# Attention and experts: shared weights added once to all 16 experts, experts' sums fetched per step from DRAM, values and experts' columns trimmed from 64 to 47

## The chip, the cores and the metric

The kernel runs on one core of one Trainium2 chip. The metric is the device time in microseconds (us). The engines of the core are TensorE (PE; its weight loads are PEld), VectorE (DVE), ScalarE (ACT), GpSimd (POOL) and SyncE (SP), which here only issues transfers. They run their own instruction streams and wait for each other by semaphores.

## The reference

64 images of 64x64x3 pass through a spectral network, which gives 64 tokens of width 64 per image; 77 text tokens per image are embedded and put behind them. So each image has 141 tokens. Then:

```
h = h + attention(layernorm(h))          # 8 heads of 8, mask: 7x7 neighbourhood on a grid of 11
h = h + ffn(layernorm(h))
# ffn, per image, with e = route_id[image]:
f = relu(x @ Wi.T + bi)                  # 64 -> 128
for l in range(2):
    shared = f @ Ws[l].T + bs[l]
    routed = f @ Wr[l, e].T + br[l, e]   # one of 16 experts
    f = relu(shared + routed + f)
out = f @ Wo.T + bo                      # 128 -> 64
```

The change lies in the attention and in this last network alone. All is float32.

## The kernel before

`token_network` makes the tokens and writes them to DRAM (about 2645 of the 3238 us). `attention_and_experts` then takes them two images (a pair) at a time, 32 pairs. The 141 tokens of an image are three blocks of BLK = 47 queries (b0, b1, b2), each against KEYS = 119 keys. The two images of a pair lie on partitions 0 to 46 and 64 to 110, so tiles have 64 slots an image of which 47 are used.

Each engine has its own written-out order of work, `step(i, p, b)`, called for each couple i, pair p of it and block b by `each_step`: couples 0 and 1 unrolled, a loop over the middle ones, the last one and a drain unrolled. `at(i, p, b, lag)` gives the work item that lies `lag` blocks back; in one step three pairs are in progress: `here` (scores, mask, softmax, values), `prev` one pair behind (output of attention, residual, second layer norm) and `old` two pairs behind (the network with the experts). `num(i, p)` is the pair's number.

The work of a step, by engine:

- TensorE: `turn` (transposes of the softmax, L1775), `back_o` (L1800), `back_layer` (both layers of the experts, L1829), `back_out` (L1836), `scores` (L1764), `front1` (L1735), `values` (softmax times values, L1788), `back_y` (L1815), `front2` (L1742, L1743), `back_in` (input matmul, L1820), `front3` (L1750), `back_proj` (projection, L1806). In block b1's part of the order stand: turn of b0, back_o, layer 0, scores of b2, values of b0, front3, back_proj, layer 1.
- VectorE: `with_mask` (scores + mask, PSUM to SBUF, L2015), `row_max` (L2025), `norm_end` (L1998), `o_norm` (L2031, L2034), `weights` (L2055), `residual` (L2043), `norm` (L1985 to L1994), `final` (L2064).
- GpSimd: `shift` (subtracts the row's maximum, L2124), `keys` (L2118), `power` (L2107, L2109), `with_bias` (L2131).
- ScalarE: `exp` (L1907), copies out of PSUM (L1886 to L1921), ReLUs (L1925, L1931).
- SyncE: tokens of pairs ahead (`xs`, `xr`, L1691) and results out (L1716).

`weights` stands in VectorE's order in block b1 of the step, between the row maximum of b1 and the mask addition of b2. For each of the two images it reads the image's expert number into a register and adds the shared weights `ws` (the identity for "+ f" is put into them once, L2072) to that expert's slice of `wr`, which holds all 16 in SBUF, [128, 2 layers, 16 experts, 129]; 128 weights and a bias. The sum goes to `wc[p]`. `wc_ready` lets TensorE begin layer 0 of that pair a step later.

The values are matmuls with the transposed softmax stationary, 64 columns an image of which 47 are queries, and 9 moving columns a head (8 values and a column of ones for the sum). Input matmul, layers and output matmul also run over all 64 slots an image.

Of the kernel before, what the change touches and what calls it, by code (L numbers as in the profile page):

```python
# [1545 lines left out]
BLK = TOK // 3  # L1546
# [8 lines left out]
def attention_and_experts(nc, t, tokens, out):  # L1555

    with ExitStack() as ctx:
# [58 lines left out]
        p_ps = ps[0:KEYS, 2:4, :]  # L1616
        o_ps = ps[:, 4, 0:3 * HEADS * (HD + 1)]
        fr_ps = [ps[:, 5, :], ps[:, 6, :]]
        ff_ps = ps[:, 7, :]
# [44 lines left out]
        f_ready = sem("f_ready")  # L1664
        wc_ready = sem("wc_ready")
        y_psr = sem("y_psr")
# [17 lines left out]
        def _(sp):  # L1684
# [13 lines left out]
            sp.wait_ge(t_setup, 4)  # L1698

            def step(i, p, b):  # L1700
                if b == 0 and at(i, p, 0, 0):
# [5 lines left out]
                if b == 0 and at(i, p, 0, 0) and (c := at(i, p, 0, -6)):  # L1707

                    sp.wait_ge(xn_ready, num(i, p) + 1)
                    waits_apart(sp, t_passed)  # L1710
                    load(xs[p], c[0], c[1], xs_in[p])
                if b == 0 and (c := at(i, p, 0, 9)):
                    sp.wait_ge(fin_ready, num(c[0], c[1]) + 1)
                    waits_apart(sp, t_passed)
                    for m in range(2):
                        sp.dma_start(out[bass.ds(2 * num(c[0], c[1]) + m, 1)].rearrange("a (b r) d -> (a r) b d", b=3),  # L1716
                                     fin[c[1]][64 * m:64 * m + BLK]).then_inc(fin_out[c[1]], 16)
# [5 lines left out]
        def _(pe):  # L1723
            pe.wait_ge(t_const, 16 * len(loads))
            pe.wait_ge(t_zero, 4)
            pe.wait_ge(t_setup, 6)
# [52 lines left out]
            def values(i, p, b):  # L1779
# [5 lines left out]
                for h in range(HEADS):  # L1785
                    for m in range(2):
                        o = (HEADS * b + h) * (HD + 1)
                        last = nc.tensor.matmul(o_ps[64 * m:64 * m + 64, o:o + HD + 1],  # L1788
                                                pT[:, h, 64 * m:64 * m + 64], vv[p][:, m, b, h, :],
                                                start=True, stop=True)  # L1790
# [27 lines left out]
            def back_in(i, p):  # L1818
                pe.wait_ge(yT_ready, num(i, p) + 1)
                nc.tensor.matmul(ff_ps[:, 0:384], wi[:], yT[:].rearrange("d b n -> d (b n)"),  # L1820
                                 start=True, stop=True).then_inc(f_psr, 1)

            def back_layer(i, p, l):
                g = num(i, p)
                pe.wait_ge(f_ready, 3 * g + l + 1)
                if l == 0:
                    pe.wait_ge(wc_ready, g + 1)
                for m in range(2):
                    last = nc.tensor.matmul(ff_ps[:, 192 * m:192 * m + 192], wc[p][:, l, m, 0:HID], ff[l][:, :, m, :],  # L1829
                                            start=True, stop=True)  # L1830
                last.then_inc(f_psr, 1)

            def back_out(i, p):
                pe.wait_ge(f_ready, 3 * num(i, p) + 3)
                for b in range(3):
                    last = nc.tensor.matmul(ff_ps[:, 64 * b:64 * b + 64], ff[2][:, b].rearrange("k m n -> k (m n)"), wo[:],  # L1836
                                            start=True, stop=True)
                last.then_inc(y_psr, 1)
# [39 lines left out]
        def _(act):  # L1878
            act.wait_ge(t_zero, 4)
            act.wait_ge(t_const, 16 * len(loads))  # L1880
# [42 lines left out]
            def relu_in(i, p):  # L1923
                act.wait_ge(f_psr, 3 * num(i, p) + 1)
                nc.scalar.activation(ff[0][:].rearrange("k b m n -> k (b m n)"), ff_ps[:, 0:384], ACT.Relu, bias=bi[:]  # L1925
                                     ).then_inc(f_ready, 1)

            def relu_layer(i, p, l):
                act.wait_ge(f_psr, 3 * num(i, p) + l + 2)
                for m in range(2):  # L1930
                    last = nc.scalar.activation(ff[l + 1][:, :, m, :], ff_ps[:, 192 * m:192 * m + 192]  # L1931
                                                .rearrange("k (b n) -> k b n", b=3), ACT.Relu, bias=wc[p][:, l, m, HID:HID + 1])
# [33 lines left out]
        def _(dve):  # L1966
            for p in range(2):
                nc.vector.memset(xs[p][:], 0.0).then_inc(xs_zero, 1)
            for tile in (xT, qT[0], qT[1], yT):
                nc.vector.memset(tile[:], 0.0).then_inc(t_zero, 1)  # L1970
            for p in range(2):
                nc.vector.memset(vv[p][:, :, :, :, HD:HD + 1], 1.0).then_inc(t_setup, 1)
# [75 lines left out]

            def weights(i, p):

                g = num(i, p)
                at_least(dve, y_psr, g - 1)
                for m in range(2):
                    e = dve.value_load(route[0:1, bass.ds(4 * i + 2 * p + m, 1)], min_val=0, max_val=EXPERTS - 1)
                    last = nc.vector.tensor_tensor(wc[p][:, :, m, :], wr[:, :, bass.ds(e, 1), :].rearrange("p l a n -> p l (a n)"),  # L2055
                                                   ws[:], ALU.add)
                last.then_inc(wc_ready, 1)

            def final(i, p):
# [13 lines left out]
                                    ).then_inc(t_setup, 1)  # L2073
            dve.wait_ge(t_setup, 7)

            def step(i, p, b):
# [12 lines left out]
                if b == 0 and prev:  # L2089
                    o_norm(*prev[0:2])  # L2090
                if b == 1 and prev:
                    weights(*prev[0:2])
                if b == 2 and prev:
# [193 lines left out]
```

## Time and profile before

| | |
|---|---|
| time, median of 3 runs | 3235.67 us (3233.77 to 3237.13) |
| span of the profiled execution | 3238.3 us |
| TensorE matmul busy | 2941.1 us, 91% |
| VectorE busy | 2306.9 us, 71% |
| ScalarE busy | 2158.6 us, 67% |
| GpSimd busy | 2115.6 us, 65% |
| attention and experts | from about 2649 us to the end |
| mean granted clock of TensorE | 0.964 |

The span is the profiled execution's time from the first to the last instruction; no time around it is given beside it, so it is compared with the median of the timed runs, of another execution each. Matmuls are pipelined: an instruction's duration is longer than the distance to the next one's start, which is what a sequence of them costs. The granted clock is a share of 2.4 GHz: 1.00 is that, 0.50 is 1.2 GHz. In the lines, PE, PEld, DVE, ACT, POOL are the engines, "L1829" is a line of the kernel, `pst` the PSUM tensor of this stage and `sm`, `mx`, `wc` tiles.

### The profile page before, as it was taken

To read this page: it belongs to the slowest core of one execution; us is meant where nothing else is said; L and a number is where in the kernel's file an instruction comes from. 1 tells how busy PE (TensorE), PEld (TensorE's weight loads), DVE (VectorE), ACT (ScalarE), POOL (GpSimd) and SP (SyncE) were. 2 spreads that over 40 slices of the span, in tenths; PEclk is the share of its full clock that TensorE was granted. 3 is DMA by queue.
4 is the path that set the end of the run, shared out by engine and by line. 5 is a ranking of instruction groups with operands and counts; after the bars stand their busy time and mean duration, and the time that the engine had idled before them with its cause. 6 is when DMAs were issued, how large, how long until landed. Compare 5 with 4: busy or idle time off the path is not lost. (4 is left out here: it accounts for less than half of the span.)

```text
span 3238.3 us, 190683 instructions
## 1 busy us (share of the span) xinstructions
PE 2941.1 (91%) x80542; PEld 1998.9 (62%) x80542; DVE 2306.9 (71%) x3829; ACT 2158.6 (67%) x3644; POOL 2115.6 (65%) x1147
## 2 busy tenths in 40 slices
PE   6877999997999998799999689999999969999998
PEld 4555777775777776577777434444444426777776
DVE  7766888984889886588888344444444428999996
ACT  5664777774677775477777267777777755655654
POOL 3763999993899995599999234444444425666663
PEclk9997999999999999899999789999999988999998
DMA  5764555554455554455554411111111110000000
GB/s 167 222 220 155 174 177 175 173 184 134 153 175 175 181 174 162 125 176 178 177 171 163 134 49 56 58 58 55 57 59 60 48 49 12 14 13 13 13 13 10
DMA packets 215406, 369.21 MB, mean 114 GB/s; under 512 B 116051, under 2 KB 133267, under 8 KB 215011
## 3 DMA queue, kind: packets, MB, share of 16 engines
q1 hardware_dynamic: 203602, 353.37, 34.2%
q10 hardware_dynamic: 7920, 10.03, 1.0%
q0 software_dynamic: 3744, 3.84, 0.8%
q8 instruction: 101, 1.65, 0.2%
q14 instruction: 39, 0.31, 0.0%
HBM read 209.43 MB, written 157.71 MB: 113 GB/s over the span
## 5 line engine op out<-in xcount | busy, mean ns | idle before, releaser
L1481 POOL TENSOR_TENSOR rstd<-var,mhalf 128x16 f32<-128x16 f32 x512 | 1524.3, 2993 | 689.2 <-DVE var L1238 683.7
L1238 DVE TENSOR_REDUCE var<-sq 128x16 f32<-128x528 f32 x384 | 403.5, 1052 | 87.9 <-ACT sq L903 87.3
L1252 DVE TENSOR_TENSOR zt<-ps,rstd 128x512 f32<-128x512 f32 x512 | 345.4, 684 | 77.9 <-POOL rstd L1481 71.8
L615 PEld LDWEIGHTS ps<-d,hp 128*32 128x32 f32 x24576 | 292.6, 111 | 132.0 <-ACT hp L915 98.5
L615 PE MATMUL ps<-d,hp 128*32 128x48 f32 x24576 | 345.6, 209 | 27.0 <-ACT hp L915 16.6
L544 PEld LDWEIGHTS ps<-cwl,hc 64*64 64x64 f32 x16384 | 272.8, 139 | 138.9 <-issue 132.7
L527 PE MATMUL ps<-zb,ex 48*128 48x512 f32 x1024 | 301.0, 664 | 55.8 <-DVE zt L1252 20.5
L555 PEld LDWEIGHTS ps<-dyi,gt 64*48 64x48 f32 x16384 | 230.1, 124 | 160.3 <-issue 148.7
L1074 ACT ACTIVATE a<-ps,fc1b 128x1024 f32<-128x1024 f32 x256 | 271.3, 1111 | 64.7 <-PE ps L818 64.7
L544 PE MATMUL ps<-cwl,hc 64*64 64x64 f32 x16384 | 308.5, 226 | 0.0
L903 ACT ACTIVATE sq<-ps 128x512 f32<-128x512 f32 x384 | 218.9, 598 | 129.5 <-PE ps L544 118.4
L555 PE MATMUL ps<-dyi,gt 64*48 64x32 f32 x16384 | 272.2, 210 | 34.1 <-ACT gt L969 14.4
L945 ACT COPY asb<-ps 128x384 f32<-128x384 f32 x384 | 191.5, 499 | 165.7 <-PE ps L615 165.7
L1238 DVE TENSOR_REDUCE var<-sql 128x16 f32<-128x528 f32 x128 | 141.6, 1108 | 208.3 <-ACT sql L903 208.3
L915 ACT ACTIVATE hp<-zt 128x512 f32<-128x512 f32 x384 | 231.9, 628 | 80.8 <-DVE zt L1316 80.8
L1309 DVE TENSOR_TENSOR zt<-zt,gbx 128x512 f32<-128x512 f32 x384 | 275.7, 718 | 10.2
L591 PE MATMUL ps<-ident,hp 128*128 128x128 f32 x1536 | 273.9, 301 | 6.7 <-ACT ho L929 4.9
L1316 DVE TENSOR_TENSOR zt<-zt,gbx 128x512 f32<-128x512 f32 x384 | 265.0, 690 | 10.3
L834 PE MATMUL ps<-a,fc 128*64 128x512 f32 x1024 | 254.0, 616 | 3.5 <-ACT a L1074 3.5
L2124 POOL TENSOR_TENSOR sm<-sm,mx 128x952 f32<-128x952 f32 x96 | 176.1, 1835 | 96.7 <-DVE mx L2025 96.7
L929 ACT COPY ho<-ps 128x512 f32<-128x512 f32 x384 | 223.5, 582 | 12.0 <-PE ps L591 4.3
L591 PEld LDWEIGHTS ps<-ident,hp 128*128 128x128 f32 x1536 | 202.9, 196 | 29.0 <-ACT ho L929 8.0
(198 smaller groups left out, 4999.7 us busy)
## 6 DMA issues: line engine op xcount, KB each, us to landing
h_scratch<-ho SPq DMA_DIRECT2D x256, 512.0 KB
hc<-h_scratch SPq DMA_DIRECT2D x256, 512.0 KB, 3.9
wsb<-in_w SPq DMA_DIRECT2D x64, 288.0 KB
gin<-g_scratch SPq DMA_DIRECT2D x252, 72.0 KB
gin<-g_scratch SPq DMA_DIRECT2D x504, 36.0 KB
g_scratch<-hp ACTq DMA_DIRECT2D x32, 192.0 KB, 4.8
g_scratch<-hp SPq DMA_DIRECT2D x32, 192.0 KB, 3.9
tokens<-wsb SPq DMA_DIRECT2D x256, 4.0 KB
```

Source lines behind the costliest of these rows:

```text
L527: nc.tensor.matmul(main_ps(s, h, u), ex[k], zb[b][k, h, :], start=True, stop=False, skip_group_check=True, tile_position=(64 * u, 0))
L544: last = nc.tensor.matmul(main_ps(s, h, u)[64 * m:64 * m + 64, r:512:8], hc[b][k, 8 * h + r, 64 * m:64 * m + 64], cwl[k], start=False, sto ...
L555: last = nc.tensor.matmul(z[c][64 * u:64 * u + 2 * TRIG, 32 * col:32 * col + 32], gt[b][rows, k].rearrange("k n s a -> k (n s a)"), dyi[ro ...
L591: last = nc.tensor.transpose(t_mid[:, 128 * a:128 * a + 128], src, ident[:])
L615: last = nc.tensor.matmul(a_ps[row:row + 32, 2 * TRIG * k:2 * TRIG * k + 2 * TRIG], hp[b][:, u, 8 * j + k].rearrange("p v r -> p (v r)"), ...
L834: last = nc.tensor.matmul(f2_ps[64 * v:64 * v + 64, u, :], fc2[:], a1[:, 2 * u + v, :], start=True, stop=True, tile_position=(0, 64 * v))
L1074: nc.scalar.activation(a1[:, 2 * u:2 * u + 2, :], f1_ps[:, 2 * u:2 * u + 2, :], ACT.Gelu, bias=fc1b[:]).then_inc(a1_ready, 1)
L1238: nc.vector.tensor_reduce(dst, src, axis=AX.X, op=ALU.add).then_inc(var_ready, 1)
L1252: nc.vector.tensor_tensor(by_px(zt[h][:, u]), by_px(main_ps(s, h, u)), scale, ALU.mult).then_inc(norm_ready, 1)
L1309: nc.vector.tensor_tensor(z, z, channels(s, 0).unsqueeze(2).to_broadcast([128, C, 16]), ALU.mult).then_inc(gain_ready, 1)
L1316: nc.vector.tensor_tensor(z, z, channels(s, 1).unsqueeze(2).to_broadcast([128, C, 16]), ALU.add).then_inc(zt_ready, 1)
L1481: nc.gpsimd.tensor_tensor(rstd[u][:], var[u][:], mhalf[:], ALU.pow).then_inc(rstd_ready, 1)
```

## The change

- The shared weights are added once, by one VectorE instruction ahead of the steps, to all 16 experts in place. SyncE stores the sums to DRAM (`expert_scratch`), expert by expert, and waits for the store once, at pair 1 of couple 0.
- `weights` is gone from VectorE. In its place SyncE loads each image's expert sum from DRAM to `wc[p]`, at an address from a register that it reads from `route`. These loads stand in SyncE's order behind the loads of tokens and ahead of the store of results, once the pair that used `wc[p]` before is through its output matmul. TensorE's layer 0 waits for the DMA.
- Values: 47 stationary columns an image in place of 64. The rows of PSUM that are no longer written are set to 1.0 once, and `ff[2]` to 0.
- Input matmul 282 moving columns in place of 384; each layer's matmul 141 in place of 192; output matmul 111 stationary columns in place of 128. The ReLUs write 47 of 64 slots.

```diff
+        w_dram = nc.dram_tensor("expert_scratch", [EXPERTS, 128, 2, HID + 1], F32).ap()
@@ sync
+            def store_experts():
+                sp.wait_ge(w_summed, 1)
+                sp.dma_start(w_dram.rearrange("e k l n -> k l e n"), wr[:]).then_inc(w_stored, 16)
+                sp.wait_ge(t_experts, 16 * len(expert_loads))
+                sp.wait_ge(w_stored, 16)
+
+            def load_experts(i, p):
+                at_least(sp, y_psr, num(i, p) - 1)
+                waits_apart(sp, t_passed)
+                for m in range(2):
+                    e = sp.value_load(route[0:1, bass.ds(4 * i + 2 * p + m, 1)], min_val=0, max_val=EXPERTS - 1)
+                    sp.dma_start(wc[p][:, :, m, :], w_dram[bass.ds(e, 1)].rearrange("a k l n -> (a k) l n")).then_inc(wc_in[p], 16)
...
                     load(xs[p], c[0], c[1], xs_in[p])
+                if isinstance(i, int) and i == 0 and p == 1 and b == 0:
+                    store_experts()
+                if b == 0 and (c := at(i, p, 0, 3)):
+                    load_experts(c[0], c[1])
                 if b == 0 and (c := at(i, p, 0, 9)):
@@ tensor
-                        last = nc.tensor.matmul(o_ps[64 * m:64 * m + 64, o:o + HD + 1],
-                                                pT[:, h, 64 * m:64 * m + 64], vv[p][:, m, b, h, :],
+                        last = nc.tensor.matmul(o_ps[64 * m:64 * m + BLK, o:o + HD + 1],
+                                                pT[:, h, 64 * m:64 * m + BLK], vv[p][:, m, b, h, :],
...
-                nc.tensor.matmul(ff_ps[:, 0:384], wi[:], yT[:].rearrange("d b n -> d (b n)"),
+                nc.tensor.matmul(ff_ps[:, 0:6 * BLK], wi[:], yT[:].rearrange("d b (m n) -> d (b m) n", m=2)[:, :, 0:BLK],
...
                 if l == 0:
-                    pe.wait_ge(wc_ready, g + 1)
+                    pe.wait_ge(wc_in[p], 32 * (i + 1))
                 for m in range(2):
-                    last = nc.tensor.matmul(ff_ps[:, 192 * m:192 * m + 192], wc[p][:, l, m, 0:HID], ff[l][:, :, m, :],
-                                            start=True, stop=True)
+                    last = nc.tensor.matmul(ff_ps[:, 3 * BLK * m:3 * BLK * m + 3 * BLK], wc[p][:, l, m, 0:HID],
+                                            ff[l][:, :, m, 0:BLK], start=True, stop=True)
...
-                    last = nc.tensor.matmul(ff_ps[:, 64 * b:64 * b + 64], ff[2][:, b].rearrange("k m n -> k (m n)"), wo[:],
-                                            start=True, stop=True)
+                    last = nc.tensor.matmul(ff_ps[0:64 + BLK, 64 * b:64 * b + 64], ff[2][:, b].rearrange("k m n -> k (m n)")[:, 0:64 + BLK],
+                                            wo[:], start=True, stop=True)
@@ scalar: relu_in and relu_layer read 6 * BLK and 3 * BLK columns and write slots 0:BLK
@@ vector
-            for tile in (xT, qT[0], qT[1], yT):
+            for tile in (xT, qT[0], qT[1], yT, ff[2]):
                 nc.vector.memset(tile[:], 0.0).then_inc(t_zero, 1)
+            nc.vector.memset(o_ps, 1.0).then_inc(t_zero, 1)
...
-            def weights(i, p):
-                g = num(i, p)
-                at_least(dve, y_psr, g - 1)
-                for m in range(2):
-                    e = dve.value_load(route[0:1, bass.ds(4 * i + 2 * p + m, 1)], min_val=0, max_val=EXPERTS - 1)
-                    last = nc.vector.tensor_tensor(wc[p][:, :, m, :], wr[:, :, bass.ds(e, 1), :].rearrange("p l a n -> p l (a n)"),
-                                                   ws[:], ALU.add)
-                last.then_inc(wc_ready, 1)
...
             dve.wait_ge(t_setup, 7)
+            nc.vector.tensor_tensor(wr[:], wr[:], ws[:].unsqueeze(2).to_broadcast([128, 2, EXPERTS, HID + 1]), ALU.add
+                                    ).then_inc(w_summed, 1)
...
-                if b == 1 and prev:
-                    weights(*prev[0:2])
```

## Rows read from the trace of the kernel before

**Rows 1.** Busy us by engine in a stretch; then granted clock, DMA share, GB/s
```profile
2900.00:2950.00 50.00, 48.07 (x571) 36.50 (x567) 45.44 (x73) 29.62 (x50) 31.44 (x31) 1.00 0.06 13
```

**Rows 2.** Chain of work in order of time: start us, us, what
```profile
2896.72 1.13 PE pst L1775 x8
...
2913.71 1.13 PE pst L1775 x8
2915.17 0.65 PE pst L1829 x4
2915.82 0.96 PE pst L1764 x8
2916.79 1.03 PE pst L1788 x32
...
2930.39 1.13 PE pst L1775 x8
```

**Rows 3.** Timeline of the same steps: start us, us, engine, line, idle before
```profile
2902.76 1.78 POOL L2124 TENSOR_TENSOR sm<-sm,mx 128x952 f32<-128x952 f32 x1 [1.33 <-DVE mx L2025]
...
2914.38 2.97 DVE L2055 TENSOR_TENSOR wc<-wr,ws 128x258 f32<-128x258 f32 x2
...
2917.27 1.14 DVE L2015 TENSOR_TENSOR sm<-pst,mask 128x952 f32<-128x952 f32 x1
...
2919.66 1.77 POOL L2124 TENSOR_TENSOR sm<-sm,mx 128x952 f32<-128x952 f32 x1 [1.33 <-DVE mx L2025]
...
2920.08 0.36 DVE L2043 TENSOR_TENSOR h<-pst,xr 128x192 f32<-128x192 f32 x1 [0.50 <-PE pst L1806]
...
2920.87 0.60 DVE L1987 TENSOR_SCALAR mu<-st 128x3 f32<-128x3 f32 x1
...
2922.93 0.17 DVE L1987 TENSOR_SCALAR mu<-st 128x3 f32<-128x3 f32 x1
...
2924.21 1.14 DVE L2015 TENSOR_TENSOR sm<-pst,mask 128x952 f32<-128x952 f32 x1
```

**Rows 4.** Timeline of TensorE in the network before: 32 and 48 stationary columns
```profile
1000.60 0.89 PE L615 MATMUL ps<-d,hp 128*32 128x48 f32 x64
1001.42 0.65 PE L555 MATMUL ps<-dyi,gt 64*48 64x32 f32 x40
```

**Rows 5.** Timeline of the stage's start: VectorE behind its loads, SyncE
```profile
2654.68 0.23 DVE L1980 TENSOR_SCALAR hmask<-hmask,temp 128x4 f32<-128x4 f32 x1 [2.15 <-DMA mask<-in_mask]
...
2671.25 0.43 DVE L2072 TENSOR_TENSOR ws<-ws,identt 128x256 f32<-128x256 f32 x1 [6.93 <-DMA wr<-in_wr]
...
2671.71 1.15 DVE L2015 TENSOR_TENSOR sm<-pst,mask 128x952 f32<-128x952 f32 x1
...
2679.37 3.96 SPq L1691 DMA_DIRECT2D xs<-tokens  x2
```

**Rows 6.** SyncE's issues in a step; DMA issues: KB, us to landing
```profile
2922.59 3.73 SPq L1691 DMA_DIRECT2D xs<-tokens  x2
...
tokens<-emb SPq DMA_DIRECT2D x1, 624.0 KB, 4.9
```

**Rows 7.** Step 1: timelines of VectorE and TensorE, and stretches as in rows 1
```profile
2693.99 2.73 DVE L2055 TENSOR_TENSOR wc<-wr,ws 128x258 f32<-128x258 f32 x2
...
2693.08 1.13 PE L1775 MATMUL pst<-identt,sm 128*119 128x128 f32 x8 [0.84 <-ACT sm L1907]
...
2694.47 1.03 PE L1764 MATMUL pst<-km,qT 64*64 64x476 f32 x8
...
2712.41 1.04 PE L1775 MATMUL pst<-identt,sm 128*119 128x128 f32 x8
...
2691.00:2697.00 6.00, 5.16 (x64) 3.62 (x61) 5.79 (x7) 3.50 (x6) 4.61 (x4) 1.00 0.00 0
...
2703.00:2709.00 6.00, 4.16 (x45) 2.51 (x45) 3.75 (x7) 1.41 (x2) 3.71 (x5) 0.69 0.08 18
```

**Rows 8.** Chain of work in the drain, at half clock
```profile
3214.30 1.65 PE pst L1829 x4
```

More of the change, by code:

```diff
@@ L1664, in attention_and_experts @@
         f_ready = sem("f_ready")
-        wc_ready = sem("wc_ready")
+        w_summed = sem("w_summed")
+        w_stored = sem("w_stored")
+        wc_in = [sem(f"wc_in{p}") for p in range(2)]
         y_psr = sem("y_psr")
@@ L1724, in _ @@
             pe.wait_ge(t_const, 16 * len(loads))
-            pe.wait_ge(t_zero, 4)
+            pe.wait_ge(t_zero, 6)
             pe.wait_ge(t_setup, 6)
@@ L1878, in _ @@
         def _(act):
-            act.wait_ge(t_zero, 4)
+            act.wait_ge(t_zero, 6)
             act.wait_ge(t_const, 16 * len(loads))
@@ L1924, in relu_in @@
                 act.wait_ge(f_psr, 3 * num(i, p) + 1)
-                nc.scalar.activation(ff[0][:].rearrange("k b m n -> k (b m n)"), ff_ps[:, 0:384], ACT.Relu, bias=bi[:]
-                                     ).then_inc(f_ready, 1)
+                nc.scalar.activation(ff[0][:].rearrange("k b m n -> k (b m) n")[:, :, 0:BLK],
+                                     ff_ps[:, 0:6 * BLK].rearrange("k (c n) -> k c n", n=BLK), ACT.Relu, bias=bi[:]).then_inc(f_ready, 1)
             def relu_layer(i, p, l):
@@ L1930, in relu_layer @@
                 for m in range(2):
-                    last = nc.scalar.activation(ff[l + 1][:, :, m, :], ff_ps[:, 192 * m:192 * m + 192]
+                    last = nc.scalar.activation(ff[l + 1][:, :, m, 0:BLK], ff_ps[:, 3 * BLK * m:3 * BLK * m + 3 * BLK]
                                                 .rearrange("k (b n) -> k b n", b=3), ACT.Relu, bias=wc[p][:, l, m, HID:HID + 1])
```

## The prediction

> **What bounds the kernel now.** The edit touches only the last stage, so I read the busy time by stretch first. In a stretch of the attention loop TensorE is busy 48.07 of 50 us at full clock, VectorE 45.44, GpSimd 31.44, ScalarE 29.62 [rows 1]. Two engines near the top say little about which of them ends a step; the chain of work in order of time does. One step (one pair of images, three blocks b0 to b2) runs there from a transpose (L1775) of block b0 to the next. The reader is to see that the chain goes through TensorE from 2913.71 to just ahead of VectorE's `h` at 2920.08 (transpose, experts' layer 0, scores of b2, values of b0, L1750, projection), crosses to VectorE for the residual and two layer norms, to GpSimd for the power and the shift, to ScalarE for the exponential, and back [rows 2]. Two steps in a row start at 2896.72, 2913.71 and 2930.39: 16.99 and 16.68 us, mean 16.83.
>
> The third view is the timeline of the engines beside that chain [rows 3]. The `mu` of L1987 takes 0.60 us there, and a second one 0.17 us later on the same shape. The long one starts at 2920.87, while GpSimd's shift of block b2 (L2124) runs from 2919.66 to 2921.43, and ends at 2921.47: it is held until GpSimd is done. In the step before, GpSimd's shift from 2902.76 ends at 2904.54, and there too the chain goes on just behind it. So the end of GpSimd's shift of b2 sets the step, not the projection that the chain names. That shift comes 2.39 us behind the start of VectorE's mask addition (L2015) of b2, and the addition starts at 2917.27, directly behind the experts' addition (L2055), though its scores (TensorE, 2915.82 + 0.96) were ready at 2916.78.
>
> **The change part by part.**
>
> *Experts' addition off VectorE.* It removes two L2055 instructions a step, 2.97 us together, held by GpSimd in their turn, and two register loads. Only 0.45 to 0.6 us of it stands before the mask addition of b2; the rest lay where VectorE had no work in reach. GpSimd's work beside these additions may become shorter, off the chain.
>
> *Trimmed columns.* A layer's two matmuls are four instructions of 192 columns in 0.65 us [rows 2], 0.85 ns a column; 51 fewer give 4 x 51 x 0.85 = 0.17 us a layer, and the same for the input matmul (2 x 102 x 0.85). Layer 0 stands on the chain ahead of the scores of b2. Layer 1, the input and the output matmul stand in TensorE's other half of the step, off the chain.
>
> *Together.* With T the start of the b0 transpose, the scores of b2 end at T + 3.07 - 0.17 = 2.90; mask addition from 2.93; shift 2.39 later at 5.32, ending at 7.09; `mu` 0.04 behind it at 7.13. Before it was 7.76 in one step and 7.85 in the other: 0.63 and 0.72 earlier, mean 0.68. All behind `mu` (VectorE's chain to the mask addition at 2924.21, GpSimd, ScalarE) depends on nothing that stays late, and moves along: TensorE has spare time at the end of the step. A step of 16.15 us follows.
>
> *Values with 47 stationary columns.* 32 instructions take 1.03 us, 32 ns each [rows 2], with 9 moving columns, so nearly all of it is loading 64 stationary ones. The nearest row is L615: 64 instructions with 32 stationary and 48 moving columns from 1000.60 to the next line's start at 1001.42, 12.8 ns each [rows 4]. On a straight line between the two, 47 columns would cost 22 ns; at one column a cycle of full clock, 25 ns; unchanged, 32. I take 25, so 0.23 us a block, with 0 and 0.33 as ends; that 47 is no round number could also cost, which I bound at +0.1 (the 119-column transposes run at 1.13 us for 8, so odd widths are nothing unusual here). In the steady loop it is worth nothing either way: `mu` could start at T + 7.16 - 0.17 - 0.23 = 6.76, or 6.99 with no gain, and waits for GpSimd until 7.09 in both.
>
> The Trainium skill has a rule against this edit, in "TensorE: Matmul & The Clock Gate", section "Wait — 56ns, not 53.3ns?": start to start, matmuls do not come closer than some 25 ns however few columns move. By it the saving ends at (32 - 25) x 32 = 0.23 us a block, as I take it; the trace has 12.8 ns between instructions of four column tiles [rows 4], so the rule does not hold for tiled ones. By the one or the other the sum stays within 1.5 us.
>
> *Sum of shared and routed weights, once.* One VectorE instruction of 2 x 16 x 129 = 4128 elements. Mask addition and `h`, 952 in 1.14 and 192 in 0.36 us, give 1.03 ns an element and 0.16 fixed: 4.4 us. Ends: 16 times the 256 elements of L2072 (0.43 us) would be 6.9; at two elements a cycle, as a one-input form might run, half, 2.2. It stands right where VectorE has waited for the last load: `ws` at 2671.25 and at 2671.71 the first mask addition, which all of the loop follows [rows 5]. Nothing covers it: +4.4. The two added memsets (384 elements and 216, some 0.7 us at 1.03 ns and the fixed part) stand ahead of VectorE's wait of 2.15 us for the mask, which hides them; without that wait they would cost their 0.7.
>
> *Store and loads through DRAM on SyncE.* SyncE is held by earlier issues until 2683.3 [rows 5], so the store (2.1 MB, 4096 runs of 516 bytes) starts there, not behind the sum. The tokens' store, 2496 runs of 256 bytes, lands in 4.9 us [rows 6]; by count 8 us, by doubling it for the bytes 16. It ends at 2691 to 2699. SyncE's next transfers wait for `h` of step 1 anyway, which comes behind that step's experts' addition (2693.99 + 2.73, and 4.4 later now), and pair 0's experts are wanted 1.5 us into step 2, at 2712.41 + 1.5 + 4.4 = 2718 [rows 7]. In the loop SyncE issues xr and xs until about 2926.3, then now two register loads and two DMAs (some 4 us by the xs row, 3.73 for two), so the store of results behind them comes some 3 us later [rows 6]; it is waited for two pairs later. A pair's experts are asked for over 20 us before their layer 0. Cost: nothing; if a transfer took over 20 us all of this would come onto TensorE.
>
> *First and last steps.* In step 1 the experts' addition runs at 2693.99 for 2.73 us, while scores of b2 are ready at 2694.47 + 0.96 = 2695.43: the mask addition comes 1.1 us earlier [rows 7]. Step 2 waits for TensorE; I give 0.3. The last full step and the drain go by TensorE and latency: 1.0 for step 30 (two layers, three values at 0.23, rounded), and 3.1 behind it: five input and layer calls at half clock (a layer is 1.65 us there with its tail, [rows 8]) at 2 x 0.17, two layers at full clock, three values, and 0.3 for shorter ReLUs and output.
>
> Sum: of the 32 steps, 0 to 31, those from 3 to 29 are steady ones; 27 x 0.68 = 18.4, + 1.1 + 0.3 + 1.0 + 3.1 = 23.9 earlier, 4.4 later: 19.5 us off the span of 3238.3, to 3218.8. That span is 2.6 us above the median of the timed runs, 3235.67; the ratio 0.9940 gives 3216.
>
> **The rivals.**
>
> *Only TensorE's trimming counts (3230).* If TensorE, 96% busy, is the real bound and the hold of `mu` an accident, a step gets shorter by 0.17 alone: 27 x 0.17 + 4.4 of the ends - 4.4 + 1 = about 5.6 us. For it: TensorE's share [rows 1]. Against: a 0.60 us `mu` beside one of 0.17, and less TensorE work would shorten a TensorE-bound step by 0.51 to 1.2 us, not 0.17, so even this rival may end near 3220.
>
> *More comes (3208).* In step 1 the granted clock is 0.69 in a stretch behind a wait of TensorE, and that step took 19.3 us, 2693.08 to 2712.41 [rows 7]. With the mask addition 1.1 us earlier this fall may not come: 2.5 us; with values at 0.33 and a cheaper sum (2.2) the total is some 8 us more.
>
> *Slower: the clock falls in every step (3280).* TensorE gets 0.5 us less work from the layers and 0.7 from the values in a step that shrinks by 0.68, so its idle time grows from 0.6 to about 1.1 us, with some 0.7 of it in one piece before the transpose of b0. If that lets the granted clock fall to 1.2 GHz once in a step, as in step 1, each costs about 2.5 us; 8 such steps eat the gain, 27 give +67 - 19.5, 3283. Against it: in stage-wide stretches with TensorE busy 5.16 of 6 us the clock stayed at 1.00 [rows 7], and the fall there followed a wait of some 2 us.
>
> *The transfer does not pay or arrive.* Late experts would stall layer 0; with a lead of 20 us I give it little, priced with the slower cases.
>
> **How the numbers follow.** Forecast 0.66 (own range 3209 to 3224), trimming only 0.13, more 0.12, clock 0.05, late experts or 47 columns slower than 64 by 0.4 us a block 0.04. A measurement here tells 0.2%, 6.5 us, from no change: faster means below 3229.2. The trimming rival lies half on each side. Faster 0.83, same 0.11, slower 0.06. The range that leaves out two in ten: 3207 to 3229.
>
> **What would show it.** Right: steps of 16.1 to 16.2 us from one b0 transpose to the next; the mask addition of b2 released by TensorE's scores; `mu` still held, ending with GpSimd's shift; L1829 at 141 columns about 0.48 us for four; values about 0.8 us for 32; one VectorE instruction of 4.4 us at 2671.7. Wrong: a step within 0.2 of 16.83, the first mask addition released by something other than that sum, a layer 0 that waits for a DMA, or a granted clock below 1.00 in the loop.

## The result, and the profile after

| | before | after |
|---|---|---|
| time, median of 4 runs each | 3234.93 us (3233.77 to 3237.13) | 3217.84 us (3217.23 to 3222.97) |
| ratio, 95% interval | | 0.9947 (0.9933 to 0.9961) |
| span of the profiled execution | 3238.3 us | 3221.1 us |
| mean granted clock of TensorE | 0.964 | 0.965 |

17 us faster, 2 us above the forecast of 3216. The 4 runs of before are the 3 known ones and one beside the changed kernel. The stage lies in the two profiles as follows. T of a step is again the start of the b0 transpose, L1775 before and L1796 after.

| part of the stage | before, us | after, us | difference | predicted |
|---|---|---|---|---|
| first memset to first mask addition | 22.5 | 27.0 | +4.5 | +4.4 |
| from there to T of step 1 | 21.37 | 20.91 | -0.5 | 0 |
| step 1 | 19.33 | 15.62 | -3.7 | -1.1 |
| step 2 | 16.18 | 16.11 | -0.1 | -0.3 |
| steps 3 to 29, mean of one | 16.83 | 16.24 | -0.59, x27 = -15.9 | -0.68, x27 = -18.4 |
| step 30 | 15.76 | 14.56 | -1.2 | -1.0 |
| step 31 and drain | 39.7 | 34.8 | -4.9 | -3.1 |
| stage | 589.1 | 567.4 | -21.7 | -19.5 |

The stage gained 21.7 us and the span only 17.2, because the stage began 4.5 us later in the profiled execution of after: its first memset stands at 2653.72 us, against 2649.19 before. The code ahead of it is the same, and over all profiles of this study the stage begins anywhere from 2643.9 to 2658.8 us. That profiled execution is also the slowest of the four of after, 3222.97 us. The experiments below are therefore read by the length of the stage and of the steps, and their times only by the ratio.

Line numbers moved: mask addition L2015 is now L2037, row maximum L2047, `h` L2065, `mu` L2009, product with `rs` L2020, `shift` L2136, `with_bias` L2143, exponential L1928, scores L1785, values L1809, layers L1850, L1750 is L1771, projection L1827.

The chain of work after, in order of time (start us, us, what), answers to [rows 2]:

```profile
2912.14 1.13 PE pst L1796 x8
2913.27 0.33 PE pst L1821 x3
2913.60 0.48 PE pst L1850 x4
2914.08 0.96 PE pst L1785 x8
2915.04 0.81 PE pst L1809 x32
2915.85 1.39 PE pst L1771 x12
2917.24 0.68 PE pst L1827 x6
...
2918.90 0.44 DVE mu L2009
...
2925.39 1.79 POOL sm L2136
2927.20 1.01 ACT sm L1928
2928.20 0.04 issue
2928.24 1.13 PE pst L1796 x8
```

A layer's four instructions take 0.48 us (0.65 before), the 32 of the values 0.81 (1.03), and this step 16.10 us. It has the same links as before, so the chain still seems to go through TensorE and the projection.

The timeline of the same step tells otherwise, as it did in [rows 3] (start us, us, engine, line, operation, idle before and its releaser):

```profile
2915.11 1.15 DVE L2037 TENSOR_TENSOR sm<-pst,mask 128x952 f32<-128x952 f32 x1 [2.40 <-PE pst L1785]
2917.52 1.78 POOL L2136 TENSOR_TENSOR sm<-sm,mx 128x952 f32<-128x952 f32 x1 [1.13 <-DVE mx L2047]
2918.12 0.36 DVE L2065 TENSOR_TENSOR h<-pst,xr 128x192 f32<-128x192 f32 x1 [0.68 <-PE pst L1827]
2918.90 0.42 DVE L2009 TENSOR_SCALAR mu<-st 128x3 f32<-128x3 f32 x1
2920.79 0.17 DVE L2009 TENSOR_SCALAR mu<-st 128x3 f32<-128x3 f32 x1
2922.07 1.14 DVE L2037 TENSOR_TENSOR sm<-pst,mask 128x952 f32<-128x952 f32 x1
2923.45 0.59 POOL L2143 TENSOR_TENSOR h1b<-h,bo 128x192 f32<-128x192 f32 x1
2923.51 0.74 DVE L2020 TENSOR_TENSOR xn<-xn,rs 128x192 f32<-128x192 f32 x1
```

VectorE now waits 2.40 us for TensorE's scores before the mask addition of b2. The mask addition starts at T + 2.97, where it had started at T + 3.56 behind the experts' addition. GpSimd's shift ends at 2919.30, T + 7.16, and `mu`, begun 0.42 us before, ends at 2919.32. The last two rows show a second hold that I had not read in the profile of before: `with_bias` on GpSimd starts at 2923.45, and the product for `xn`, which takes 0.36 us elsewhere, takes 0.74 beside it (the two end at 2924.04 and 2924.25). In every other step the product for `yn` is the one beside `with_bias`; it takes 0.67 us there and the one for `xn` 0.34. The row maximum, and so the next shift, stands behind both.

The start of the stage after answers to [rows 5]; its `SPq` rows are SyncE's issues:

```profile
2675.87 0.43 DVE L2084 TENSOR_TENSOR ws<-ws,identt 128x256 f32<-128x256 f32 x1 [7.14 <-DMA wr<-in_wr]
2676.33 4.46 DVE L2087 TENSOR_TENSOR wr<-wr,ws 128x4128 f32<-128x4128 f32 x1
2680.71 1.14 DVE L2037 TENSOR_TENSOR sm<-pst,mask 128x952 f32<-128x952 f32 x1
...
2687.67 1.95 SPq L1705 DMA_DIRECT2D expert_scratch<-wr  x1
...
2704.25 2.01 SPq L1715 DMA_DIRECT2D wc<-expert_scratch  x2
```

The sum takes 4.46 us right ahead of the first mask addition. The store is issued at 2687.67 and the first load of expert sums, which waits for it, at 2704.25: the store took at most 16.6 us with its issue, and no layer 0 waits for it (pair 0's starts at 2718.5). A later pair's load lands in 2.7 us by the page's row of DMA issues.

### The profile page after: what moved, and what is told of

It is laid out like the page before. It is cut to its first block and busy times, and to the rows that moved or that the text cites. A ratio compares the mean times of both kernels' runs of the same rounds, so it can differ in the third digit from the quotient of the medians.

```text
span 3221.1 us, 190782 instructions
## 1 busy us (share of the span) xinstructions
PE 2893.1 (90%) x80542; PEld 1961.7 (61%) x80542; DVE 2215.7 (69%) x3767; ACT 2148.5 (67%) x3644; POOL 2102.1 (65%) x1147
## 5 line engine op out<-in xcount | busy, mean ns | idle before, releaser
L1309 DVE TENSOR_TENSOR zt<-zt,gbx 128x512 f32<-128x512 f32 x384 | 275.4, 717 | 10.2
L2136 POOL TENSOR_TENSOR sm<-sm,mx 128x952 f32<-128x952 f32 x96 | 170.5, 1776 | 94.7 <-DVE mx L2047 94.7
```

Of the source, the lines that this page charges most:

```text
L1309: nc.vector.tensor_tensor(z, z, channels(s, 0).unsqueeze(2).to_broadcast([128, C, 16]), ALU.mult).then_inc(gain_ready, 1)
```

## The experiments

Stages and steps are those of each kernel's own profile, times are medians, and each ratio is to the kernel before on the same chip (several chips were used, so times of different rows don't compare to the last microsecond). "Mean step" is the mean of steps 3 to 29, each from one profile; in the second profiles of after and all_three it came out the same. The changed kernel's ratio was 0.9947 in one measurement and 0.9922 in the other, so differences of a few us between its variants show in steps and stages only.

| kernel | time, us | ratio (95%) | mean step | stage |
|---|---|---|---|---|
| before | | | 16.83 | 589.1 |
| after | 3217.84 | 0.9947 (0.9933 to 0.9961) | 16.24 | 567.4 |
| move_only | 3227.66 | 0.997 (0.9957 to 0.9983) | 16.40 | 576.3 |
| trim_only | 3238.97 | 1.0015 (1.0001 to 1.0028) | 17.01 | 588.3 |
| values64 | 3220.67 | 0.9957 (0.9945 to 0.9968) | 16.23 | 570.5 |
| values32 | 3222.21 | 0.996 (0.9945 to 0.9976) | 16.32 | 571.4 |
| layers_only | 3239.47 | 1.0001 (0.9991 to 1.0012) | 17.10 | 592.1 |
| mu_from_psum | 3215.34 | 0.9922 (0.9906 to 0.9939) | 16.04 | 563.9 |
| bias_later | 3211.35 | 0.9905 (0.9889 to 0.9922) | 15.89 | 557.2 |
| late_sum | 3218.52 | 0.9932 (0.9915 to 0.9948) | 16.17 | 564.2 |
| all_three | 3197.79 | 0.9884 (0.9859 to 0.9909) | 15.58 | 546.9 |
| all_three_v64 | 3207.69 | 0.9894 (0.9874 to 0.9914) | 15.78 | 558.7 |
| after, again | 3213.48 | 0.9922 (0.9904 to 0.9939) | 16.24 | 567.9 |
| all_three, again | 3197.3 | 0.9873 (0.9855 to 0.989) | 15.58 | 547.9 |

**The move alone (move_only).** The changed kernel with every trimmed column given back.

```diff
-  nc.tensor.matmul(o_ps[64 * m:64 * m + BLK, ...], pT[:, h, 64 * m:64 * m + BLK], ...)
+  nc.tensor.matmul(o_ps[64 * m:64 * m + 64, ...], pT[:, h, 64 * m:64 * m + 64], ...)
   # likewise 384, 192 and 128 columns in the input, layer and output matmuls and in the ReLUs
```

> The experts' addition is moved as in the change; values, input, layer and output matmuls keep their 64 slots (the ReLUs too). My theory: a step is set by the end of GpSimd's shift of block b2, which follows the scores of b2. Layer 0 is 0.17 us longer, so the step goes from 16.24 to 16.41 us; start, step 30 and drain lose what trimming gave there (about 5 us). Time about 3227 to 3229. Rival (TensorE's trimming is what counts, the addition only came off an engine with spare time): the step is that of before, 16.83 us, and with the sum's 4.4 us the time is 3235 to 3239.

The mean step was 16.40 us. So the experts' addition off VectorE is worth 0.43 us a step by itself, of 0.59, and the rival by which only the trimming counts is out. Its `mu` was hardly held, though, by the timeline of move_only:

```profile
2915.69 1.78 POOL L2135 TENSOR_TENSOR sm<-sm,mx 128x952 f32<-128x952 f32 x1 [1.29 <-DVE mx L2046]
2916.51 0.36 DVE L2064 TENSOR_TENSOR h<-pst,xr 128x192 f32<-128x192 f32 x1 [0.90 <-PE pst L1827]
2917.29 0.20 DVE L2008 TENSOR_SCALAR mu<-st 128x3 f32<-128x3 f32 x1
```

GpSimd's shift ends at 2917.47 and `mu` begins 0.18 earlier: with the old widths the way over TensorE and `h` and the way over GpSimd are late together. That is why the layers' trimming, which shortens both, gives 0.17 on top, and the values' trimming, which shortens the first alone, nothing.

**The trimming alone (trim_only).** The experts' addition back on VectorE, no copy in DRAM, all columns trimmed.

```diff
+                if b == 1 and prev:
+                    weights(*prev[0:2])
...
-            nc.vector.tensor_tensor(wr[:], wr[:], ws[:].unsqueeze(2).to_broadcast(...), ALU.add).then_inc(w_summed, 1)
...
-                if b == 0 and (c := at(i, p, 0, 3)):
-                    load_experts(c[0], c[1])
```

> All columns trimmed as in the change; the experts' addition stays on VectorE where it was. My theory: the mask addition of b2 stays behind the experts' addition, not behind the scores, so a step gains little, 16.65 to 16.83 us; without the sum's 4.4 us and with the shorter drain the time is 3225 to 3230. If the second of the two additions slips in ahead of GpSimd's shift of b1, VectorE is free earlier and the step is near 16.3: then about 3214. Rival (trimming alone makes the gain): step 16.24 us, time about 3213.

The expected time of 3225 to 3230 us was missed: it took 3238.97 us, no faster than before. The expected step of 16.65 to 16.83 us came in the ordinary steps, 16.7 and 17.0 us, as before to the tenth; the timeline of trim_only shows why trimming gave nothing:

```profile
2926.92 1.13 PE L1775 MATMUL pst<-identt,sm 128*119 128x128 f32 x8 [0.58 <-ACT sm L1907]
...
2927.36 3.28 DVE L2056 TENSOR_TENSOR wc<-wr,ws 128x258 f32<-128x258 f32 x2
...
2928.79 1.03 PE L1764 MATMUL pst<-km,qT 64*64 64x476 f32 x8
...
2930.57 1.14 DVE L2016 TENSOR_TENSOR sm<-pst,mask 128x952 f32<-128x952 f32 x1
...
2932.96 1.78 POOL L2125 TENSOR_TENSOR sm<-sm,mx 128x952 f32<-128x952 f32 x1 [1.33 <-DVE mx L2026]
...
2933.68 1.09 DVE L1988 TENSOR_SCALAR mu<-st 128x3 f32<-128x3 f32 x1
```

The scores of b2 begin 0.17 us earlier (T + 1.87; T + 2.04 in the timeline of before), and the mask addition still starts at T + 3.65, behind the experts' addition; `mu` only stands longer in its hold, 1.09 us. Beyond that, four steps took 17.9, 19.4, 19.3 and 19.4 us, each at a fall of the granted clock. The step behind each was 0.67 us shorter than its like, so the four cost 0.2 to 1.7 us each and 5.3 together, more than step 30 and the drain gained by the trimming (4.1). Here is one, by stretch (columns as in [rows 1]):

```profile
2880.00:2896.00 16.00, 14.21 (x187) 10.57 (x186) 15.21 (x24) 9.77 (x17) 10.27 (x10) 1.00 0.06 14
2896.00:2903.00 7.00, 6.29 (x79) 5.12 (x77) 6.42 (x14) 3.58 (x7) 3.59 (x6) 1.00 0.04 9
2903.00:2913.00 10.00, 9.25 (x71) 6.31 (x75) 8.04 (x11) 4.45 (x9) 5.85 (x5) 0.66 0.07 15
```

TensorE was busy 14.21 of 16 us and 6.29 of 7 at 2.4 GHz, then the clock fell to 1.2 GHz for part of ten. The timeline of TensorE shows what stood ahead of the fall:

```profile
2901.24 1.13 PE L1775 MATMUL pst<-identt,sm 128*119 128x128 f32 x8
2903.75 1.79 PE L1764 MATMUL pst<-km,qT 64*64 64x476 f32 x8 [1.38 <-DVE sm L2016]
```

The scores waited 1.38 us for VectorE's mask addition and then took 1.79 us in place of 1.03. This is the fall that I had named for the slower rival, but behind another wait: I had looked for it at the idle time before the transpose of b0. It came in four steps of 27, in a kernel whose steps VectorE ends.

**The values alone at 64 (values64)**, the first diff without its comment line, and **at 32 (values32)**, where the output of queries 32 to 46 of each block is left out:

```diff
-  nc.tensor.matmul(o_ps[64 * m:64 * m + BLK, ...], pT[:, h, 64 * m:64 * m + BLK], ...)
+  nc.tensor.matmul(o_ps[64 * m:64 * m + 32, ...], pT[:, h, 64 * m:64 * m + 32], ...)
```

> The changed kernel with 64 stationary columns in the values again. My theory: nothing in the steady step (16.24 us), since the mu of the second layer norm waits for GpSimd anyway; start, last step and drain lose 0.22 us a block, 1.5 to 2 us in all: 3219 to 3220. Rival (the values stand on the chain): 0.22 us a step, 3224; if TensorE is the bound, three times 0.22 a step, 3235.

> The changed kernel with 32 stationary columns in the values; rows 32 to 46 of each block are left out of the attention's output. If loading goes by the column at full clock (64 columns 1.03 us, 47 columns 0.81 us for 32 instructions), 32 columns take about 0.61 us; if matmuls keep a distance of 25 ns, it stays near 0.80 us. Steady step 16.24 us by my theory in both cases, time within 2 us below 3217.8; if the values stood on the chain, 0.2 us a step less, 3212.

With 64 columns the mean step is 16.23 us, that of after: in the loop the values' trimming earns nothing. The timeline of values64 shows where it goes:

```profile
2912.31 0.20 DVE L2009 TENSOR_SCALAR mu<-st 128x3 f32<-128x3 f32 x1
```

T is 2905.32 there and GpSimd's shift ends at 2912.48. `mu` begins at T + 6.99, 0.23 us later than in after (6.76), and ends at 7.19, as in after (7.18). What the trimming earns lies at the ends, 0.7 us in step 30 (15.25 against 14.56). Step 31 and the drain take 37.3 us against 34.8, but that is mostly the clock: it fell 11.3 us into that part in values64 and 18.6 us into it in after. In mu_from_psum, which has 47 columns and whose clock fell 10.8 us into it, the part takes 37.2. The intervals of the ratios, 0.9957 and 0.9947, overlap. The distance from the first values matmul to the next line's start gives the cost of a width; in values32's timeline of TensorE:

```profile
3090.89 0.68 PE L1809 MATMUL pst<-vv,pT 119*32 119x9 f32 x32
3091.50 1.46 PE L1771 MATMUL pst<-wv,xT 128*119 128x64 f32 x12
```

That is 0.61 us for 32 instructions, 19 ns each; 47 columns take 0.81 us, 25 ns, and 64 take 1.03, 32 ns. The three lie on one line: 0.41 ns a column and some 6 ns fixed. The rule of the Trainium skill in "TensorE: Matmul & The Clock Gate", section "Wait — 56ns, not 53.3ns?", by which starts never come closer than about 25 ns, doesn't hold for these instructions, which put the outputs of the two images on partitions from 0 and from 64 in turn (two column tiles). The ordinary steps of values32 are 16.1 and 16.4 us; its mean of 16.32 comes from one step of 18.5, with a fall of the clock at 3100.

**Which trimming lets the clock fall (layers_only).** My theory after trim_only was that the values' trimming opened the gaps. This kernel trims only the input, layer and output matmuls, with the addition on VectorE.

```diff
   # trim_only, with
-  nc.tensor.matmul(o_ps[64 * m:64 * m + BLK, ...], pT[:, h, 64 * m:64 * m + BLK], ...)
+  nc.tensor.matmul(o_ps[64 * m:64 * m + 64, ...], pT[:, h, 64 * m:64 * m + 64], ...)
```

> Only the input, layer and output matmuls trimmed; values with 64 columns, the experts' addition on VectorE where it was. In trim_only the granted clock fell four times in the loop, in steps of 17.9 to 19.4 us, where TensorE had 15.0 us of work in 16.83. My theory: the values' 0.66 us a step of less work opened those gaps while VectorE kept the step at 16.83; with 64 columns the clock stays at 1.00 in the loop, steps 16.83, and the time is 2 to 4 us below the kernel before. Rival (the falls came from the shorter layers or from chance in the chip): falls of the clock in this loop too, time at or above the kernel before.

The theory was wrong: there are three falls again, at 2906, 3043 and 3081 us, for 6.8, 10.2 and 6.8 us. The stretches that follow show the busy times over the same 350 us of five kernels, with the columns of [rows 1]; TensorE's is the first after the length, the granted clock the third from the end.

In trim_only:

```profile
2750.00:3100.00 350.00, 313.32 (x3918) 235.05 (x3917) 326.59 (x493) 201.64 (x351) 218.91 (x207) 0.98 0.06 13
```

In layers_only:

```profile
2750.00:3100.00 350.00, 326.55 (x3886) 248.67 (x3885) 314.32 (x493) 199.04 (x343) 215.80 (x206) 0.97 0.06 13
```

In values32:

```profile
2750.00:3100.00 350.00, 308.91 (x4135) 230.00 (x4135) 268.74 (x477) 211.22 (x365) 219.32 (x218) 1.00 0.13 29
```

In after:

```profile
2750.00:3100.00 350.00, 321.91 (x4137) 243.40 (x4137) 262.50 (x475) 212.33 (x369) 219.85 (x216) 1.00 0.13 29
```

In all_three:

```profile
2750.00:3100.00 350.00, 334.26 (x4281) 252.71 (x4280) 261.66 (x490) 221.41 (x385) 229.00 (x226) 1.00 0.13 31
```

Busy share alone doesn't tell which kernel falls: layers_only does with 326.55 us (part of it at half clock, which lengthens it), after doesn't with 321.91. The waits do tell more. Here is the one at the first fall in layers_only:

```profile
2906.37 1.82 PE L1764 MATMUL pst<-km,qT 64*64 64x476 f32 x8 [1.08 <-DVE sm L2016]
```

All eight falls in these loops (four in trim_only, three in layers_only, one in values32) began within 2 us of the end of such a wait of the scores for a mask addition, of 1.07 to 1.47 us; seven of them within 0.3 us. In the loops of before, after, move_only, values64, mu_from_psum, bias_later, late_sum, all_three and all_three_v64, which have no fall, no wait of TensorE was longer than 0.94 us. But waits of 1.07 us and more stand in every step or every other step of the three kernels that fell, and mostly the clock stayed. What else must meet there is open. So is how often each kernel falls, as most have one profile.

**The hold of `mu` (mu_from_psum).** The three sums that `mu` reads go to a free corner of PSUM.

```diff
-        st2 = sb("st2", [128, 3])
...
+        st2 = ps[:, 5, 400:403]
```

> The changed kernel; the sums over a row in the second layer norm are written to a free corner of the PSUM bank of the projection, so that mu's instruction reads PSUM and not SBUF. My theory: mu is held in the changed kernel by GpSimd's shift of b2 (it starts 6.76 us into the step and ends at 7.18, 0.04 behind the shift), because both use the same way into SBUF; reading PSUM it is not held and ends at about 6.95 to 7.0. Step 16.24 to 16.02 us, time about 6 us below the changed kernel. Rival (mu's 0.4 us have another cause, or GpSimd's work behind the shift sets the step): step 16.24, no change of time.

The timeline of this kernel:

```profile
2911.77 1.78 POOL L2136 TENSOR_TENSOR sm<-sm,mx 128x952 f32<-128x952 f32 x1 [1.12 <-DVE mx L2047]
...
2913.15 0.16 DVE L2009 TENSOR_SCALAR mu<-pst 128x3 f32<-128x3 f32 x1
```

`mu` ends at 2913.31, 0.24 us before GpSimd's shift does (2913.55), and the mean step falls by 0.20 us to 16.04. So the hold was real, and it set the step in the changed kernel. The time alone wouldn't show it: 0.9922 is also what the changed kernel measured the second time. The Trainium skill, "SBUF — State Buffer", section "Who interferes with whom", has the rule behind it: VectorE and GpSimd share a pair of SBUF ports that one of them takes for a whole instruction, and `tensor_scalar` can be of the kind that needs it. The trace agrees: 0.42 us beside the shift with the operand in SBUF, 0.16 with it in PSUM; a `mu` from SBUF with no shift beside it takes 0.17.

**The second hold (bias_later).** GpSimd adds `bo` to `h` behind the next shift of b0 instead of ahead of it.

```diff
+                if b == 0 and (c := at(i, p, 0, 6)):
+                    with_bias(*c[0:2])
...
-                if b == 2 and prev:
-                    with_bias(*prev[0:2])
```

> The changed kernel; GpSimd's with_bias (h1b, 0.59 us) of a pair is moved from the end of its step to behind the shift of b0 of the next, where GpSimd waits 1.4 us for the copy of the keys. My theory: it holds the multiplications of L2020 (yn or xn, 0.67 to 0.74 us in place of 0.36) on the chain, so 0.3 to 0.37 us a step goes: step near 15.9 us, time 8 to 10 us below the changed kernel. Rival (the multiplication would wait for the power anyway): step 16.24, no change.

The mean step fell by 0.35 us to 15.89, and both products take their plain time in this kernel's timeline, in both kinds of step. Here is one:

```profile
2922.61 1.14 DVE L2037 TENSOR_TENSOR sm<-pst,mask 128x952 f32<-128x952 f32 x1
2923.67 0.35 DVE L2020 TENSOR_TENSOR yn<-yn,rs 128x192 f32<-128x192 f32 x1
2924.05 0.36 DVE L2020 TENSOR_TENSOR xn<-xn,rs 128x192 f32<-128x192 f32 x1
```

By the same section of the Trainium skill a VectorE instruction with two SBUF inputs contends with a GpSimd instruction that reads SBUF, and these rows agree, 0.74 us beside `with_bias` and 0.36 without. The second hold was worth more than the first, and 0.59 us of GpSimd work of no urgency had only to be moved behind the next shift.

**The sum later (late_sum).** The sum stands behind the row maximum of b1 in step 0, where VectorE has a gap.

```diff
-            nc.vector.tensor_tensor(wr[:], wr[:], ws[:].unsqueeze(2).to_broadcast(...), ALU.add).then_inc(w_summed, 1)
...
+                if isinstance(i, int) and i == 0 and p == 0 and b == 1:
+                    nc.vector.tensor_tensor(wr[:], wr[:], ws[:].unsqueeze(2).to_broadcast(...), ALU.add).then_inc(w_summed, 1)
```

> The changed kernel; the sum of 4128 elements is moved from ahead of the first mask addition to behind the row maximum of b1 in step 0, where VectorE waits 4.32 us for TensorE. My theory: the 4.46 us are hidden there, start to first mask addition 22.5 us as before the change, 4 to 4.5 us less in all, the same steps. Rival (the clock of TensorE or the store to DRAM eats it): less than 2 us.

The first mask addition came 22.2 us into the stage (27.0 in after), but T of step 1 then 22.87 us behind it (20.91): 4.82 won and 1.96 given back. VectorE's timeline in late_sum:

```profile
2685.11 4.45 DVE L2100 TENSOR_TENSOR wr<-wr,ws 128x4128 f32<-128x4128 f32 x1
2690.28 1.15 DVE L2037 TENSOR_TENSOR sm<-pst,mask 128x952 f32<-128x952 f32 x1 [0.73 <-PE pst L1785]
```

VectorE waits again behind the sum, so that place covers it, at least in part. In that stretch, 2685 to 2700, the granted clock is 0.72: it is at 1.2 GHz until 2690, the end of a stretch of 34 to 38 us that every profile here has at the stage's start, and falls again for 3.4 us at 2693. Of the four profiles with the sum at this place, three have such a fall ahead of step 1 (3.4, 10.2 and 3.4 us), and of the others none; whether the place causes it is open. all_three has none, and its T of step 1 still lies 22.12 us behind the first mask addition.

The stage is 3.2 us shorter, which the time can't tell from after. Only 2.9 of that is gained up to T of step 1. The mean step is 0.07 us shorter too, 16.17, though nothing in the loop was changed: in every other step VectorE's wait put down to "issue" ahead of the mask addition of b0 is 0.14 us and not 0.36. No run shows why. That gives 1.8 us; step 1 takes back 0.25 and the drain, with an earlier fall of the clock, 1.2.

**All three together (all_three, run twice), and with 64 columns (all_three_v64).** The three diffs above in one kernel; the second also has the values64 diff. The first version beat both kernels, so it was run again beside the changed kernel.

> mu from PSUM, with_bias later and the sum later, together, in the changed kernel. If the three are independent places of one chain: step about 15.7 us, time 18 to 20 us below the changed kernel, about 3198 to 3200 against 3217.8. If TensorE becomes the bound or its granted clock begins to fall in the loop: step above 16, time above 3206.

> all_three with 64 stationary columns in the values. Theory (values are off the chain in the loop): steps within 0.03 us of all_three's 15.58, start, last step and drain 1.5 to 3 us longer, no fall of the clock in the loop: time 1 to 4 us above all_three. Rival (with the shorter step the values have come onto the chain): 0.2 us a step or more, 6 us and more above all_three.

> all_three again, for its ratio in the same call as the changed kernel: 0.987 to 0.990 of the kernel before, 0.993 to 0.995 of the changed one; steps 15.58 us.

> The changed kernel again, on the chip of the others of this call: ratio to the kernel before 0.993 to 0.996, steps 16.24 us, the stage of attention and experts 567 us in its profile. The span ahead of that stage may differ by some us, as it did between profiles.

all_three takes 3197.3 us against 3213.48 for the changed kernel beside it, 0.9950 of it, and the two ratios to before, 0.9873 (0.9855 to 0.989) and 0.9922 (0.9904 to 0.9939), don't overlap. Its mean step of 15.58 us was the same in both runs. The three edits together give 0.66 us a step. One by one they gave 0.20, 0.35 and, from the place of the sum, 0.07: 0.62, so they nearly add up. TensorE is busy 334.26 of 350 us at full clock. With 64 columns the step is 15.78: once both holds are gone, most of the values' 0.23 us is on the path that sets the step, and the rival expectation for this run came true. That kernel's stage is 11.8 us longer than all_three's, but only 27 x 0.2 = 5.4 of that is in the steps; much of the rest is a fall of the clock for 10.2 us at 2690, in the start.

## Why the prediction was right, point by point

- **GpSimd's shift of b2 ends the step, through `mu`.** Right. In after `mu` ends 0.02 us behind the shift, and mu_from_psum takes 0.20 us off the step. The mask addition of b2 is released by the scores, as said.
- **0.68 us a step.** The mechanism was right, the size too large by 0.09: 0.59, so the mean step is 16.24 us and not 16.15. `mu` ends at T + 7.18 in the step shown, not at 7.13, as mask addition and shift each begin some hundredths later behind their releasers than I took. I had also let everything behind `mu` move along. In every other step VectorE's last wait, put down to "issue", ahead of the mask addition of b0 is 0.36 us; before it was 0.23. With 27 steps this term was 2.5 us too large, the largest miss on that side.
- **Layers 0.17 us.** Right, 0.65 to 0.48; and it came onto the step in full only because the addition was moved: alone it gave nothing (trim_only, layers_only).
- **Values 0.23 us a block, nothing of it in the loop.** Right: 1.03 to 0.81, and values64 has the same step.
- **The sum, +4.4 us, with nothing to cover it.** Right: 4.46. A later place covered it in part, for 2.9 us up to T of step 1. The two memsets come to some 0.9 us by the prediction's own figures, not 0.7; they were hidden all the same, as the start grew by 4.5 and no more.
- **Store and loads cost nothing.** Right. The store took at most 16.6 us, against 8 to 16 foreseen. A pair's experts are asked for some 20 us ahead of their layer 0, as said; for pair 0 it is 14 (2704.25 and 2718.5).
- **Step 1, -1.1.** Mis-sized: -3.7. The fall of the granted clock in step 1 of before [rows 7] didn't come: the stretch 2701 to 2717 stands at 1.00. That is the 2.5 us which I had put with the rival "more comes". Nor does it come in trim_only (16.67 us from 2689.97 to 2706.64) and layers_only (16.68), whose VectorE still has the experts' addition in that step. So the clock can stay up there without the earlier mask addition, which that rival had as the reason. Against these two kernels the step is 1.05 us shorter, which is the 1.1 of the sum; the rest is a fall that the one profile of before had and none of the later ones has in this step.
- **Drain, -3.1.** Mis-sized: -4.9. I had priced the layer calls there at half clock before and after. In after the clock held until 18.6 us into step 31 and the drain, to about 3205, so several ran at full clock; before it fell 11.8 us into them. Where it fell as early with all columns trimmed (mu_from_psum, 10.8 us in), this part takes 37.2 us, 2.5 less than before. So some 2.4 of the 4.9 us is the clock, and the trimming itself gave less than the 3.1 foreseen. By stretch, after:

```profile
3186.00:3205.00 19.00, 14.06 (x180) 11.30 (x179) 10.27 (x21) 9.77 (x19) 6.37 (x8) 1.00 0.09 22
3205.00:3215.00 10.00, 6.13 (x19) 4.00 (x19) 1.11 (x3) 2.26 (x6) 0.41 (x1) 0.50 0.03 7
```

- **The clock in the loop.** 1.00 in all of after. The slower rival did not come here, but the chance of it was no fancy: trim_only, layers_only and values32 have such falls. The steps hit were 0.5 to 3.1 us longer than their like.

That the total fits is in part luck. The errors on the two sides nearly cancel: 2.5 us too much in the steady steps, 4.7 too little in the other parts, most of it from the clock (19.5 foreseen, 21.7 measured in the stage). In the two profiled executions the later start of the stage took back 4.5 us of the 21.7; where the stage began in the other executions isn't known, and the second measurement of the changed kernel gave 0.9922 in place of 0.9947.

## What to carry to other kernels

When two engines look full, ask for the same small instruction at two places: one that takes 0.60 us here and 0.17 there names the engine it is held by, and the end of that engine's work is what the step hangs on, whatever the chain says. Shortening work ahead of something that already waits is worth nothing until the later wait is removed: the same trimming gave 0.17 us a step after the move and none before it, and it lengthened waits around which the clock fell. When a hold has been found, look for the next one in the same list, long next to short on one shape; the second, a bias addition placed one instruction too early, was worth more than the first.

## What the runs showed of the hardware

- The granted clock can fall to 1.2 GHz inside a steady loop with TensorE busy 309 to 327 of 350 us: four times in the loop of trim_only, three in layers_only, once in values32, for 3.4 to 10.2 us each. Each fall came at a wait of TensorE of 1.07 to 1.47 us; the kernels here whose loops have no wait above 0.94 us had none.
- A VectorE `tensor_tensor` with both inputs in SBUF (the product for `xn`) is held by GpSimd's `tensor_tensor` as `mu` is: 0.74 us beside `with_bias`, 0.36 alone.
- In two column tiles, with 9 moving columns, a matmul costs 0.41 ns per stationary column and some 6 ns: 19, 25 and 32 ns at 32, 47 and 64 columns.
- A store of 2.1 MB from SBUF to DRAM in 4096 runs of 516 bytes took at most 16.6 us with its issue; 129 KB at an address from a register landed in 2.7 us.
